# Attention of a macaron layer: each score computed once with queries on partitions, probabilities turned on TensorE before the product with V

## The reference, cut to what matters

```python
x = x + 0.5 * ffn(layernorm(x))
x = x + attn(layernorm(x))
x = x + 0.5 * ffn(layernorm(x))

def attn(x, wq, wk, wv, wo):            # q, k, v: 16 heads of 64
    q, k = rope(x @ wq.T), rope(x @ wk.T)
    scores = einsum('bhid,bhjd->bhij', q, k) * HEAD_DIM ** -0.5
    probs = softmax(where(causal, scores, -inf), axis=-1)
    out = einsum('bhij,bhjd->bhid', probs, v)
    return out.reshape(batch, seq, 1024) @ wo.T
def rope(x1, x2):                       # halves of a head
    return concat(x1 * cos - x2 * sin, x1 * sin + x2 * cos)
```

## Time and profile before

| | |
|---|---|
| median of three runs | 1344.22 us (1341.71 to 1344.45) |
| profiled execution | 1344.47 us, its span 1342.6 us |
| TensorE busy | 1284.2 us, 96% |
| VectorE busy | 874.2 us, 65% |
| GpSimd busy | 752.1 us, 56% |
| ScalarE busy | 619.0 us, 46% |
| DMA queue of SyncE | 112832 packets, 163.43 MB, 47.8% of 16 engines |
| granted TensorE clock, mean | 0.976 |

### The profile page before, as it was taken

The page is one execution under the profiler, slowest core; times in us unless marked ns, Lnnn a source line. Parts: engine busy times, 40 slices in busy tenths (PEclk is TensorE's granted clock), DMA queues, the critical chain, the costliest instruction groups (busy, mean ns, idle before and its releaser), DMA issues. The chain is left out here.

```text
span 1342.6 us, 24933 instructions
## 1 busy us (share of the span) xinstructions
PE 1284.2 (96%) x6240; PEld 734.8 (55%) x6240; DVE 874.2 (65%) x2270; ACT 619.0 (46%) x1176; POOL 752.1 (56%) x454
## 2 busy tenths in 40 slices
PE   4986799999999999999999999999999999999798
PEld 2543455555555555555555556555655555554365
DVE  5566667676767666776767676767676767664254
ACT  3655244444444444444444444444444444444474
POOL 5133256666666666666666565666666666665300
PEclk8998689999999999999999999999999999999799
DMA  7123816464656565655556465646464646452001
GB/s 274 41 94 102 190 45 158 112 158 113 158 119 158 119 158 120 158 119 139 139 124 154 111 161 117 158 108 163 105 161 106 162 103 163 106 116 50 0 24 40
DMA packets 113340, 164.81 MB, mean 123 GB/s; under 512 B 13344, under 2 KB 63392, under 8 KB 113184
## 3 DMA queue, kind: packets, MB, share of 16 engines
q1 hardware_dynamic: 112832, 163.43, 47.8%
q10 hardware_dynamic: 480, 1.05, 0.4%
HBM read 36.24 MB, written 10.49 MB: 35 GB/s over the span
## 5 line engine op out<-in xcount | busy, mean ns | idle before, releaser
L979 POOL TENSOR_TENSOR psum_p<-psum_p,shared_a 128x256 f32<-128x256 f32 (+1 forms) x192 | 280.7, 1462 | 101.4 <-ACT shared_a L807 92.7
L807 ACT ACTIVATE shared_a<-bank 128x512 f32<-128x512 f32 (+3 forms) x512 | 201.5, 445 | 235.6 <-PE bank L662 228.0
L645 PE MATMUL bank<-k_hh,q_hl 128*128 128x512 f32 (+3 forms) x768 | 257.4, 390 | 11.0 <-DVE max_all L937 8.4
L662 PE MATMUL bank<-q_hm,k_l 65*128 65x512 f32 (+3 forms) x768 | 244.8, 373 | 0.0
L869 DVE TENSOR_REDUCE max_left<-bank 128x1 f32<-128x512 f32 x256 | 175.5, 688 | 96.8 <-PE bank L645 96.8
L656 PE MATMUL bank<-q_hl,k_hh 128*128 128x512 f32 (+3 forms) x768 | 227.5, 350 | 6.7 <-DMA q_hm<-neg_max_rows 6.7
L645 PEld LDWEIGHTS bank<-k_hh,q_hl 128*128 128x128 f32 x768 | 138.2, 193 | 174.7 <-issue 73.7
L807 ACT ACTIVATE probs_more<-bank 128x512 f32<-128x512 f32 (+1 forms) x256 | 132.2, 568 | 195.5 <-PE bank L662 182.5
L873 DVE CUSTOM_DVE_ANT_0 max_scratch<-bank,tri_mask,max_left 128x128 f32<-128x128 f32 (+3 forms) x256 | 138.1, 548 | 109.4 <-PE bank L645 109.0
L682 PE MATMUL bank<-shared_a,v_cur 128*64 128x512 f32 (+3 forms) x1024 | 202.7, 474 | 0.0
L103 POOL TENSOR_TENSOR parts<-rotated,parts 128x1024 fp32r<-128x1024 f32 x64 | 152.4, 2381 | 50.3 <-ACT parts L97 50.3
(11 more groups left out here) (128 smaller groups left out, 1919.1 us busy)
## 6 DMA issues: line engine op xcount, KB each, us to landing
q_hl<-parts SPq DMA_DIRECT2D x254, 128.0 KB, 2.8
k_hh<-parts SPq DMA_DIRECT2D x254, 128.0 KB, 2.7
v_cur<-shared_b SPq DMA_DIRECT2D x32, 512.0 KB, 6.0
k_l<-parts SPq DMA_DIRECT2D x63, 256.0 KB, 4.2
q_hm<-parts SPq DMA_DIRECT2D x63, 256.0 KB, 4.9
xn_cur<-xn_scratch SPq DMA_DIRECT2D x15, 1024.0 KB, 5.8
w_qk<-w_scratch SPq DMA_DIRECT2D x32, 256.0 KB, 3.1
w_scratch<-first_w_parts SPq DMA_DIRECT2D x8, 512.0 KB, 3.1
```

The lines of the kernel that those rows point to most:

```text
L645: nc.tensor.matmul(max_bank[k % 2][:, 0:w], q_hl[u][h][:, q * P:(q + 1) * P], k_hh[u][h][:, keys * CHUNK:keys * CHUNK + w], start=True, st ...
L662: nc.tensor.matmul(scores[h][:, x0:], k_l1[u][h][:, keys], q_hm[u][h][:, q], start=False, stop=True).then_inc(scores_full, 1)
L807: nc.scalar.activation(probs_of(s)[:, h, x0:], scores[h][:, x0:], ACT.Exp, scale=SCORE_SCALE).then_inc(probs_done, 1)
L979: last = nc.gpsimd.tensor_tensor(acc, acc, new, ALU.add)
```

## The change

- Each score is computed once, with 128 queries on partitions. A unit is one block of queries of one head against all keys it may see, 128 to 1024 columns in a pair of PSUM banks (`wide_banks`). The eight blocks form two groups, `TILES` (0, 1, 6, 7) and (2, 3, 4, 5). The first group of a pair is computed during the second half of the pair before.
- The scale and a minus sign are in the q columns of the cos and sin tables. DVE adds the mask, writes the scores to SBUF and keeps each row's minimum in one instruction (`max_of`); ACT takes the exponential in place and keeps the row's sum (`exponential`, with `accum_out`).
- Probabilities now have the queries on partitions. For the product with V each block of 128x128 is turned by `nc.tensor.transpose` into one of two PSUM banks, the ring (`turn`), and copied to SBUF (`keep_turned`): 72 blocks in a pair, in 20 tiles; ACT copies 17 tiles, DVE three. `RING` gives each tile its place in the ring; the turned sums (8 blocks) and the products with the output weights use the same ring.
- `times_v` takes the keys in twos, seven times in a pair instead of twelve.
- POOL no longer adds probabilities. It takes over the last addition of the rotation (`sum_half`), the rounding, and the spreading of the inverted sums (`spread`). The maxima's products, their DMA, the operand `q_hm`, the mask products and the sums by a matrix of ones are gone. The rest of k is now in an operand of 128 rows, half of them zero.

```diff
@@ rope_unit
-    nc.vector.tensor_tensor(bank[:, w:2 * w], bank[:, 0:w], o.cos[:, cols], ALU.mult).then_inc(o.by_cos_done, 1)
-    nc.vector.tensor_tensor(bank[:, 0:w], bank[:, 0:w], o.sin[:, cols], ALU.mult).then_inc(o.by_sin_done, 1)
...
-    nc.vector.tensor_tensor(o.rotated[c][:, 1, to], bank[:, w:2 * w], o.terms[:, 1, to], ALU.add)
...
-    nc.vector.tensor_tensor(o.rotated[c][:, 0, to], o.terms[:, 0, to], bank[:, 0:w], ALU.subtract).then_inc(o.proj_free, freed)
+    nc.vector.tensor_tensor(o.cross[:, 1, to], bank[:, 0:w], o.cos[:, cols], ALU.mult)
+    nc.vector.scalar_tensor_tensor(out=o.cross[:, 0, to], in0=bank[:, 0:w], scalar=-1.0, in1=o.sin[:, cols],
+                                   op0=ALU.mult, op1=ALU.mult).then_inc(o.proj_free, freed)
@@ attention
+        TILES = [(0, 1, 6, 7), (2, 3, 4, 5)]
...
+        RING = [[0, 1, 2, 3, 4, 5, 6, 8, 9, 10], [12, 13, 14, 15, 16, 17, 18, 19, 20, 22]]
+        RING_SUM, RING_OUT = [11, 23], [21, 7]
...
+            def score(p, i, u, g, k):
...
+                if some(unit(p, g, k) - 2):
+                    pe.wait_ge(scores_taken, unit(p, g, k) - 2)
...
+                for a, b in ((x0, min(x1, CHUNK)), (CHUNK, x1)):
+                    if b > a:
+                        out, keys = wide_banks[k % 2][:, a:b], slice(a - x0, b - x0)
+                        nc.tensor.matmul(out, q, k_hh[u][h][:, keys], start=True, stop=False)
+                        last = nc.tensor.matmul(out, q, k_low[u][h][:, keys], start=False, stop=True)
...
+            def turn(p, g, t, signals=1):
...
+                may_write(p, at)
+                for a, h in enumerate(heads):
+                    for b, r in enumerate(rows):
+                        col = P * (a * len(rows) + b)
+                        last = nc.tensor.transpose(ring[at % 2][:, col:col + P],
+                                                   probs[g][:, h, OFFSET[g][r] + j * P:OFFSET[g][r] + (j + 1) * P], ident[:])
...
+            def exponential(p, g, k):
...
+                nc.scalar.activation(own, own, ACT.Exp, bias=neg_max[g][:, col], scale=-1.0,
+                                     accum_out=sums[g][:, col]).then_inc(probs_done, 1)
...
+                nc.scalar.activation(turned[:, slot, to], ring[at % 2][:, 0:w * len(heads)],
+                                     ACT.Copy).then_inc(ring_free[at % 2], signals)
...
+            def max_of(p, g, k):
...
+                nc.vector.tensor_tensor_reduce(out=part_of_probs(g, k), in0=wide_banks[k % 2][:, x0:x1],
+                                               in1=tri_mask[:, SEQ - (x1 - x0):], scale=1.0, scalar=3e38, op0=ALU.add,
+                                               op1=ALU.min, accum_out=neg_max[g][:, col]).then_inc(scores_taken, 1)
```

More of the change, by code:

```diff
@@ L747, in _, with ahead, ahead_v, next_score @@
-            pe.wait_ge(zeros_done, 2)
-            for k in range(4):
-                max_unit(0, 0, 0, k)
+                def ahead(n):
+                    if has_next2:
+                        project(i + 1, u, n)
+                def ahead_v(n):
+                    if has_next2 and u == 0:
+                        project_v(i + 1, n)
+                def next_score(k):
+                    if has_next:
+                        score(p + 1, i + u, 1 - u, 0, k)
+                turn(p, 0, 0)
@@ L835, in _, with ahead_v, next_exponential @@
-            act.wait_ge(proj_free, 6)
+                has_prev, has_next, has_next2 = not (first and u == 0), not (last and u == 1), not last
+                def ahead_v(n):
+                    if has_next2 and u == 0:
+                        keep_v(i + 1, n, 16 * (i + 1))
+                def next_exponential(k):
+                    if has_next:
+                        exponential(p + 1, 0, k)
+                exponential(p, 0, 7)
+                keep_turned(p, u, 0, 0)
+                keep_turned(p, u, 0, 1)
@@ L843, in _ @@
                 keep_first_v(n)
-            for c in range(2):
-                round_high(0, 1, c, ahead=True)
+            for k in range(7):
+                exponential(0, 0, k)
             for u in range(2):
@@ new lines, in pair @@
+                max_of(p, 1, 0)
+                max_of(p, 1, 1)
+                invert(p, 0)
+                ahead(0)
+                keep_turned(p, u, 0, 3)
+                if has_prev:
+                    normalise(p - 1, 1)
+                max_of(p, 1, 2)
+                max_of(p, 1, 3)
+                ahead(1)
+                max_of(p, 1, 4)
+                max_of(p, 1, 5)
+                if has_prev:
+                    add_to_x((2 * i + u - 1) // PAIRS, 1, RING_OUT[1], p)
+                ahead(2)
@@ new lines, in pair @@
+                max_of(p, 1, 6)
+                max_of(p, 1, 7)
+                ahead(3)
+                next_max(0)
+                ahead(4)
+                next_max(1)
+                keep_turned(p, u, 1, 3)
+                normalise(p, 0)
+                invert(p, 1)
+                next_max(2)
+                ahead(5)
+                next_max(3)
+                next_max(4)
+                keep_turned(p, u, 1, 7)
+                next_max(5)
+                add_to_x(i // (PAIRS // 2), 0, RING_OUT[0], p)
```

725 lines of the change are left out of this document (348 added, 377 removed).

## The result

The changed kernel takes 1326.82 us (median of four runs, 1325.08 to 1330.76), the kernel before 1344.06 us in the same session. The ratio is 0.9879, with a 95% interval of 0.9852 to 0.9907: faster by 17 us. 43 were forecast. The direction and the range hold; the size is less than half of the forecast.

A forecast was written before the change was run, and what follows sets the result against it. TensorE's instructions were taken as the bound: per pair 8.6 us removed, 5.5 added, 2.0 of waits, so 1.1 gained; 30 pairs give 33 us, the ends 10, so 1344.5 - 43 = 1301 us, range 1245 to 1385.

The forecast's parts named there:

- the price of a turned block: TensorE's cost of turning one 128x128 float32 block, taken as 0.055 us: 80 in a pair, 4.4 us.
- What leaves TensorE: Per pair, products for maxima, mask products, sum reductions, turned maxima and switches of value steps go: together 8.6 us.
- What comes: Per pair, TensorE gains 80 turned blocks at 4.4 us and 1.1 us at ring entries: 5.5 us added.
- the heads of tiles: At the start of each of 22 ring entries in a pair TensorE takes 0.05 us more: 1.1 us.
- Waits: TensorE waits where VectorE or ScalarE hands over late: 2.0 us a pair.
- five places: TensorE's waits: second tile 0.1 us, sixth tile 0.5, fifth score unit 0.3, next pair's fifth unit 0.5, turned sums 0.6.
- rival 1: Loads set the pace of turned blocks, 0.116 us each: slower, 1416 us; chance 0.20 with its milder forms.
- the walk: One pair without V followed through the engines' queues with the assumed prices, giving 2.0 us of TensorE waits.
- Pair: One pair in the steady loop falls from 34.4 to 33.3 us, 1.1 less, over 30 pairs 33 us.
- The switch: Each TensorE switch into float32 groups and back costs 0.30 us; five fewer in a pair save 1.5 us.
- The ends: Outside the steady loop: first pair -6 us, last pair -4, FFN halves 0; 10 us gained.
- Other engines: Busy time per pair: VectorE near 20 us, ScalarE near 22.5, GpSimd about 14; none is the bound by its sum.

The follow-up runs named there:

- the doubling: The changed kernel with every turned block of probabilities turned twice onto the same place, 72 more in a pair: 1560.8 us, ratio 1.1622 to the kernel before.
- the kernel with fewer blocks: The changed kernel with 32 of a pair's 72 probability blocks not turned from the second pair on (result not the reference's): 1277.21 us, ratio 0.9507 to the kernel before.

## Why the prediction was off

The step that failed is the price of a turned block: "I take 0.055 us, the row nearest to it". It is 0.109 (trace, and 0.102 from the doubling), which makes 80 x 0.054 = 4.3 us a pair of TensorE's work that the sum did not have. Not all of it is time: leaving out 3.5 us a pair gave 1.6 back, because cheaper blocks bring waits. The mistake was in reading: one block alone, whose next start came 0.05 us later, was taken for its whole price. The next matmul of 512 columns, from 629.51 to the value step at 629.92, took 0.41 and not the 0.33 that stand ahead of a float32 group. The missing 0.08 could have been read there. And the 140 ns of the earlier trace rows say how long a load's record is, not how closely loads can follow each other; from them I had excluded the pace of loads.

The Trainium skill, "TensorE: Matmul & The Clock Gate", section "LDWEIGHTS (loading the stationary operand)", gives 107 ns for 128 columns. The trace agrees within 2% for turned blocks: 109 ns from start to start. I had weighed this rule against the 140 ns and against one row, and gave it one chance in five.

- *What leaves TensorE*: 8.6 forecast, 10.2 found. Right in its kinds, too small in size. The surplus lies mainly in the maxima's rows, 6.1 us with their turning where I counted 4.4 by columns alone (the 0.10 ahead of value steps falls on them), and in 0.7 behind mask products, which no term had.
- *What comes*: 5.5 forecast, 9.1 found. 4.3 too little for the blocks, 0.7 too much for the heads of tiles: 0.4 a pair, and only behind value groups.
- *Waits*: 2.0 forecast, 0.8 found. Of five places one was right, with its cause and nearly its size (0.6 forecast; 0.91 and 0.30 in turn, 0.6 in the mean). Slower turning covers the others, as rival 1 said: with 32 blocks fewer there are 2.6 us a pair, at VectorE's minima, copy and addition as walked, and at a copy of ScalarE that the walk had not. The walk was sound for the price that it assumed.
- *Pair*: -1.1 forecast. The corrections are -1.6, +3.6 and -1.2, which leave -0.3; -0.34 was measured. The first is known by difference only, so this is no separate check of it.
- *Rival 1* had the mechanism right and its sum wrong: 1416 us. The block is 0.109 and not 0.116 (0.6 us a pair), the heads cost less (0.7), more leaves (1.6), and 0.1 less of the waits is covered. Together 2.8 us a pair, about 89 us.
- *The switch*: the 0.30 for each float32 group holds for value steps and sums. Output products pay none of it, as moving one showed.
- *The ends*: start -6 forecast, -4.0 found, mainly through the clock and despite TensorE's beginning 8.7 us later. Last pair -4, found -3.1. Second FFN half 0, found -3.3, also the clock: a term put at nothing because its work does not change.
- *Other engines*: ScalarE was 1.5 us a pair over the forecast. The record of its read of the accumulator lasts 188 ns (0.083 taken, "between nothing and 0.2"). The next instruction can start 0.09 behind it, though (603.97 to 604.06 in the kernel with fewer blocks), so only where ScalarE then has nothing to do is the rest added to its busy time. The 0.09 by which the record of an exponential exceeds the rounding of as many columns lies under that read:

```profile
L821 ACT ACTIVATION_READ_ACCUMULATOR probs<-probs,neg_max 128x1 f32 x512 | 96.4, 188 | 0.0
L821 ACT ACTIVATE probs<-probs,neg_max 128x1024 f32<-128x1024 f32 x64 | 73.5, 1148 | 30.0 <-DVE neg_max L932 30.0
```

It cost nothing, as moving three more copies there showed.

What stays open: how the 3.3 us of the second half would move if TensorE's idle time ahead of it were changed by itself. It was not tried apart.

## What to carry to other kernels

The price of a TensorE instruction is the distance to the next start plus what the next one takes above its own price; one short instruction alone hides its cost on its successor, so look for a row in which several follow each other, or add up a stretch. Before counting switches or groups as saved, write the new order down and see what now stands alone: regrouping value steps gave a fifth of the expected gain in one form and lost 74 us in the other, because the groups between them were what gave VectorE its time. Waits walked and prices are not independent: a price that is too low makes waits that a true one covers. And a wait can be there without idle time: where a product takes more than its price, look at the load of its successor.

## What the runs showed of the hardware

- Turned float32 blocks of 128x128 follow each other every 0.109 us, as their loads do, though a load's record lasts 140 ns; moving columns alone would have allowed about 0.06 (an estimate, half of the 0.12 for 256 columns).
- The record of ScalarE's accumulator read lasts 188 ns, but the next instruction starts 0.09 us behind it; VectorE's lasts 83 ns.
- Ahead of a group of float32 value steps (64 stationary columns) TensorE takes 0.09 to 0.10 us more; ahead of and behind a float32 product with 128 stationary columns it takes nothing more.
- The same pair of float32 matmuls of 512 columns took 2.07 us in one kernel and 1.12 in the other after an equal wait of 0.78 us; before it TensorE had waited 2.08 and 1.06 us in the one, 0.86 and 1.06 in the other. Fillers ahead of a stretch raised its granted clock from 0.73 to 0.91.
